# A gated delta-rule decoder layer with mixture of experts: one half of the batches runs 64 tokens ahead in the scan, and one pipeline takes all sixteen pairs

## Chip, cores and metric

One core of a Trainium2 chip. The metric is the device time of one execution in microseconds; the median of several runs counts.

## What is computed

The input x is 16 batches of 256 tokens of 256 features, all in f32. In the order of the reference:

1. RMS norm, a causal depthwise convolution over 4 tokens, SiLU, then projections to q, k, v (16 heads of 16) and to the gates beta and alpha.
2. The gated delta rule, token after token, per batch and head with a state S of 16 x 16: `S = a*S; pred = S.k; S = S + k (x) (beta*(v - pred)); o = S.q`. Only this part is serial in the tokens: token t needs S of token t-1.
3. Output projection and residual; RMS norm and a gated MLP with residual; layer norm of x plus all that.
4. Cross attention of the tokens over a context of 120 rows a batch, residual, layer norm.
5. A router picks one of 8 experts for each token; the expert is three matrices with two GELUs; residual, layer norm.

## The kernel before

**Units of work.** Tokens are cut into two blocks of 128 (jb 0 and 1). The batches are cut into two halves of eight (h 0 and 1), as one state instruction of VectorE holds 8 batches x 16 heads on its 128 partitions. A *pair* is two batches of one token block; there are sixteen, 0 to 7 in block 0 and 8 to 15 in block 1, of which 0 to 3 and 8 to 11 are half 0.

**The scan.** A half-token is one token of one half and takes four VectorE instructions: `state_product` (L135, S times k), `state_weights` (L147, the sum over the key axis, the value folded in as a 17th column), `state_outer` (L156), `state_update` (L166, writes S). Each needs the result of the one before it. `scan_step` writes them out by hand so that the two halves alternate: between two instructions of one half stands one of the other. The two halves share one buffer for the outer product, so the outer product of half 0 waits for half 1's update just ahead of it (a second semaphore, beside the one of its weights). `next_keys` (L113) copies four tokens of keys of both halves to PSUM, `next_values` (L118) two tokens of values of both halves. Eight tokens make a chunk (R = 8, 16 chunks a block); S of eight tokens is kept in a ring. GpSimd follows with `read_out` (L208 to L216): for four tokens of one half it multiplies S by q, folds the sum in three steps and writes the output over the values; the update waits for S to be read before it overwrites it. `store_o` sends a half's outputs of a block to memory.

**First block (front_and_scan).** PE, ScalarE, VectorE and GpSimd do part 1 for pairs 0 to 7; q, k, v and gates go through memory (`load_raw`) so that they come back with (batch, head) on the partitions. For each half VectorE then prepares: squares' sums (`sums`, L495), gates and inverse lengths (L475, L502), `normalise` of keys and queries (L513), `shares` (L480 to L486). With both halves prepared, the scan of block 0 runs: 128 tokens, all paired. Beside it the other engines do part 1 for pairs 8 to 15; `inverse_rms` of each on GpSimd stands between the read-outs of the chunks, so one pair goes with one chunk. Then the keys and values of the 16 contexts (`keys_values`). In the last two chunks VectorE does parts of the preparation of block 1; the rest stands behind the scan, since it writes into buffers that the scan reads.

**Second block (scan_and_post).** A pipeline of six stages over pairs: a mix and residual (L1088), b gate and up, f down and layer norm, c queries, scores and exponentials (VectorE: four maxima, L1113), d attention output and layer norm, e routing. In a step, stage a holds the newest pair. `PLAN = (1, 1, 1, 2, 2, 2, 2, 2, 1, 1, 1)` says how many chunks of the scan of block 1 VectorE does in each step, cut into turns of one token that stand between the stages' instructions. Pairs 0 to 7 enter in steps 0 to 7. Pairs 8 to 15 need the scan's end and enter in steps 11 to 18 (`AGAIN = M + 3`, M = 8). With the drain there are 24 steps. SP loads each pair's inputs (`load`), and for pair 8 and 9 first stores the two halves' outputs. Steps 5 to 7 and 16 to 18 are hardware loops, the others are written out.

**Then** a short block finishes the routing tables, and the experts run over 39 tiles of 128 rows; the change leaves both as they are, but for merged semaphores.

## Time and profile before

| | |
|---|---|
| median of 3 runs | 2015.93 us (2010.91 to 2018.14) |
| the profiled execution | 2012.56 us, its span 2010.9 us |
| busy over the span: PE, VectorE, GpSimd, ScalarE | 1408.4, 1274.6, 1000.1, 755.4 us |
| scan of block 0 | 118 to 537 us |
| scan of block 1 | 565 to 1085 us |
| last pair's residual | 1312 us |
| experts from | about 1460 us |

Busy time is that of instructions; VectorE's instructions overlap a little (the next can start before the last has ended), so its work is read best from start to start. The rows in order of time give start and duration in us, engine (DVE is VectorE, ACT ScalarE, POOL GpSimd, SP SyncE), line, operation, operands with shapes, and, in brackets, how long the engine was idle before and who ended it.

### The profile page before, as it was taken

How to read it: one execution, taken by the hardware profiler on the slowest of the kernel's cores; microseconds unless marked ns; L12 is line 12 of the kernel's file. 1: busy time of each engine (PE TensorE's matmuls, PEld its weight loads, DVE VectorE, ACT ScalarE, POOL GpSimd, SP SyncE). 2: the span in 40 equal slices, each digit the busy share in tenths (PEclk: the TensorE clock that was granted, in tenths of full speed). 3: DMA queues.
4: the chain of work that ended last, by engine and by line, in shares of the span. 5: the costliest groups of instructions: out<-in, count | busy, mean ns of one | idle time of the engine just before them, and what ended most of it. 6: DMA issues, size and time to landing. Idle time of an engine off the chain costs nothing. (4 is left out here: it accounts for less than half of the span.)

```text
span 2010.9 us, 28443 instructions
## 1 busy us (share of the span) xinstructions
PE 1408.4 (70%) x6660; PEld 977.0 (49%) x6661; DVE 1274.6 (63%) x3248; ACT 755.4 (38%) x2416; POOL 1000.1 (50%) x1214
## 2 busy tenths in 40 slices
PE   6504558600036676667766899998489999999997
PEld 4303336400024555545555677777345555555554
DVE  4599999999989999999986143443323223222222
ACT  5512224501103674566766577776311111111111
POOL 3238888886769987887766333341111111111111
PEclk9857778855557887878978999998789999999999
DMA  4601113610031011000002111143140420421200
GB/s 120 211 5 32 43 38 117 202 62 0 20 112 36 21 31 31 19 23 25 26 26 79 52 46 42 50 127 115 34 127 17 150 71 18 149 71 41 84 18 6
DMA packets 97685, 125.41 MB, mean 62 GB/s; under 512 B 10001, under 2 KB 74952, under 8 KB 95560
## 3 DMA queue, kind: packets, MB, share of 16 engines
q1 hardware_dynamic: 60040, 97.22, 15.3%
q10 hardware_dynamic: 33136, 18.58, 3.2%
q0 software_dynamic: 4432, 8.73, 1.2%
q8 instruction: 30, 0.49, 0.1%
q14 instruction: 47, 0.39, 0.1%
HBM read 89.68 MB, written 35.74 MB: 62 GB/s over the span
## 5 line engine op out<-in xcount | busy, mean ns | idle before, releaser
L208 POOL TENSOR_TENSOR wt<-wt 128x1024 f32<-128x1024 f32 x128 | 304.3, 2377 | 109.6 <-DVE wt L166 109.5
L214 POOL TENSOR_TENSOR wt<-wt 128x512 f32<-128x512 f32 (+2 forms) x384 | 316.9, 825 | 30.1
L1870 PE MATMUL e_ph<-wt,e_g 128*128 x624 | 274.3, 592 | 0.0
L166 DVE SCALAR_TENSOR_TENSOR wt<-wt,scan 128x256 f32<-128x256 f32 x512 | 242.2, 473 | 0.2 <-issue 0.2
L156 DVE TENSOR_TENSOR scan<-scan,wt 128x256 f32<-128x256 f32 x512 | 219.4, 429 | 20.1 <-DVE wt L166 14.0
L147 DVE TENSOR_REDUCE scan<-wt 128x16 f32<-128x272 f32 x512 | 222.6, 435 | 0.1
L135 DVE TENSOR_TENSOR wt<-wt,scan 128x256 f32<-128x256 f32 x512 | 209.5, 409 | 5.4 <-PEq L231 5.4
L1268 ACT ACTIVATE wt<-p_pX,p_mx 128x120 f32<-128x120 f32 x512 | 176.1, 380 | 89.3 <-DVE p_mx L1113 87.6
L1399 PE MATMUL p_pm<-p_w_mix,p_oT 128*128 128x256 f32 x128 | 43.5, 499 | 217.7 <-DMA p_oT<-o 188.6
L1763 POOL TENSOR_TENSOR e_ve<-e_mv,eps 128x1 f32<-128x1 f32 x39 | 7.4, 189 | 369.7 <-DVE e_mv L1814 369.7
L1870 PEld LDWEIGHTS e_ph<-wt,e_g 128*128 128x128 f32 x624 | 115.5, 190 | 130.8 <-issue 130.8
L1835 ACT ACTIVATE e_g<-e_pT 128x512 f32<-128x512 f32 x39 | 23.3, 597 | 337.9 <-PE e_pT L1885 337.9
L1908 PE MATMUL e_ph<-wt,e_xT 128*128 x312 | 149.4, 603 | 1.0 <-DVE e_xT L1785 1.0
L1792 DVE TENSOR_TENSOR e_h<-e_ph,wt 128x512 f32<-128x512 f32 x39 | 27.0, 692 | 183.4 <-PE e_ph L1870 183.4
L1399 PEld LDWEIGHTS p_pm<-p_w_mix,p_oT 128*128 128x128 f32 x128 | 30.5, 250 | 227.9 <-issue 221.4
L716 PE MATMUL f_pT<-ident,f_xn 128*128 128x128 f32 x64 | 14.9, 376 | 169.5 <-ACT f_xn L584 111.9
L1113 DVE TENSOR_REDUCE p_mx<-p_pX 128x8 f32<-128x960 f32 x64 | 72.9, 1149 | 89.0 <-PE p_pX L1442 88.8
L1410 PE MATMUL p_pX<-p_hT,p_wg 128*128 128x256 f32 (+1 forms) x384 | 108.3, 408 | 14.9 <-ACT wt L1268 14.9
L1800 DVE TENSOR_TENSOR e_h<-e_ph,wt 128x512 f32<-128x512 f32 x78 | 53.9, 692 | 101.4 <-PE e_ph L1908 99.6
L1420 PE MATMUL p_py<-p_wd,p_prod 128*128 128x256 f32 (+1 forms) x384 | 107.7, 427 | 12.5 <-DVE p_place L1168 9.1
L1268 ACT ACTIVATION_READ_ACCUMULATOR wt<-p_pX,p_mx 128x1 f32 x512 | 116.0, 226 | 0.0
L1410 PE MATMUL p_pX<-p_hT,p_wu 128*128 128x256 f32 (+1 forms) x384 | 103.0, 392 | 0.0
(220 smaller groups left out, 2977.2 us busy)
## 6 DMA issues: line engine op xcount, KB each, us to landing
wt<-in_L_ffn_W SPq DMA_DIRECT2D x24, 1024.0 KB
qkv<-f_st ACTq DMA_DIRECT2D x48, 256.0 KB, 2.3
p_kE<-kE SPq DMA_DIRECT2D x16, 480.0 KB, 3.7
p_vP<-vP SPq DMA_DIRECT2D x16, 480.0 KB
e_xt<-routed ACTq DMA_DIRECT2D x39, 130.0 KB, 2.1
f_xt<-in_x SPq DMA_DIRECT2D x16, 256.0 KB, 2.8
f_raw_k<-qkv SPq DMA_DIRECT2D x4, 1024.0 KB, 6.0
f_raw_q<-qkv SPq DMA_DIRECT2D x4, 1024.0 KB, 8.2
```

The source lines that it names most:

```text
L135: nc.vector.tensor_tensor(s["sk"][:, h, u % V, :, 0:HD], s["S"][:, h, (u - 1) % R], s["kn"][:, h, u % KN:u % KN + 1].to_broadcast([P, HD, ...
L147: nc.vector.tensor_reduce(s["w"][:, h], s["sk"][:, h, u % V], AX, ALU.add).then_inc(s["w_done"], 1)
L156: nc.vector.tensor_tensor(s["outer"][:], s["w"][:, h].rearrange("p (v o) -> p v o", o=1).to_broadcast([P, HD, HD]), s["k"][:, h, bass.ds(c ...
L166: nc.vector.scalar_tensor_tensor(s["S"][:, h, u], s["S"][:, h, (u - 1) % R], s["gate"][:, jb, h, 1, bass.ds(c * R + u, 1)], s["outer"][:], ...
L208: nc.gpsimd.tensor_tensor(x, s["S"][:, h, z * Q:(z + 1) * Q], s["q"][:, h, now].rearrange("p t (o d) -> p t o d", o=1).to_broadcast([P, Q, ...
L214: nc.gpsimd.tensor_tensor(x[:, :, :, 0:half], x[:, :, :, 0:half], x[:, :, :, half:2 * half], ALU.add).then_inc(s["o_fold"][h], 1)
L1268: ins = nc.scalar.activation(pr[:, x // 2, head], scores(x)[:, y // 4, y % 4], ACT.Exp, bias=mx[:, x // 2, head:head + 1], accum_out=sm[:, ...
L1399: ins = nc.tensor.matmul(dst[:, q], rows[:, g, q * P:(q + 1) * P], wt[:, g], start=(g == 0), stop=(g == G - 1))
L1410: ins = nc.tensor.matmul(gu(i)[0:c, which], wt[:, g, i * P:i * P + c], hT[:, g], start=(g == 0), stop=(g == G - 1))
L1420: ins = nc.tensor.matmul(py[:, q], prod[0:c, i, q * P:(q + 1) * P], wd[0:c, i], start=(i == 0), stop=(i == IC - 1))
L1870: ins = nc.tensor.matmul(ph2[:], g1[:, c // (C1 // 2), c % (C1 // 2)], wt[:, bass.ds(at_b + (W2_AT + c * F2), F2)], start=(c == 0), stop=( ...
L1908: ins = nc.tensor.matmul(ph1[:, q], xT[:, g], wt[:, bass.ds(at + (W1_AT + g * F1 + q * HALF), HALF)], start=(g == 0), stop=(g == G - 1))
```

## The change

Half 0 begins its scan as soon as it is prepared, alone (`one_step`: the four instructions of one half-token in a row). Half 1 is prepared between those steps and begins when half 0 is at token 64 (`LEAD` = 8 chunks); from then on `pair_step` alternates the two as before, half 0 at token t + 64 and half 1 at t. Since half 0 finishes a block 64 tokens before half 1, its inputs for block 1 must be there by then while the buffers still hold block 0: the preparation of block 1 writes to the freed raw buffers, `keep_next` stores that to memory (new tensor `next`) and `load_next` brings it back when the half's scan of block 0 is over. For half 0 this happens at the end of the first block, beside 8 tokens of half 1 alone, for half 1 in step 3 and 4 of the second block.

The second block does two slots of the scan (a slot is a chunk of either or both halves) in each of steps 0 to 11: slots 0 to 6 hold both (block 1 of half 0, the rest of block 0 of half 1), slot 7 half 0 alone, slots 8 to 15 both, slots 16 to 23 half 1 alone. Pairs 8 to 11 (half 0) enter in steps 8 to 11 and pairs 12 to 15 from step 12; `AGAIN` is M, and with the drain there are 21 steps. Semaphores of the scan are kept per half, key and value refills are per half and each for four tokens, and several semaphores that counted one instruction each are merged into their neighbours' (`ms_done` into `rstd_done`, `st_done` into `mv_done`, `ve_done` into `rs_done`, in all blocks), with the same instructions and waits.

The diff's core:

```diff
+LEAD = CHUNKS // 2
...
-def scan_step(nc, dve, s, jb, vo, c, u, last=False):
-    t = c * R + u
-    behind = (c, u - 1) if u else (c - 1, R - 1)
-    begun = not (isinstance(c, int) and c == 0 and u == 0)
-    state_product(nc, dve, s, jb, c, u, 0)
-    if begun:
-        state_outer(nc, dve, s, jb, *behind, 1)
-    state_weights(nc, dve, s, jb, c, u, 0)
-    if begun:
-        state_update(nc, dve, s, jb, *behind, 1)
-        if u % 2 == 0 and not (last and u == R - 2):
-            next_values(nc, s, vo, t + 2, (u - 2) % V, 2)
-    state_outer(nc, dve, s, jb, c, u, 0)
-    state_product(nc, dve, s, jb, c, u, 1)
-    state_update(nc, dve, s, jb, c, u, 0)
-    if u % KN == KN - 1 and not (last and u == R - 1):
-        dve.wait_ge(s["sk_done"], (c + jb * CHUNKS) * (2 * R) + (2 * u + 2))
-        next_keys(nc, s, t + 1)
-    state_weights(nc, dve, s, jb, c, u, 1)
...
+def updated(dve, s, at):
+    h, jb, c, u = at
+    dve.wait_ge(s["S_done"][h], (c + jb * CHUNKS) * R + (u + 1))
+def refill_keys(nc, dve, s, at):
+    h, jb, c, u = at
+    if u % KN == KN - 1 and not (isinstance(c, int) and c * R + u == TB - 1):
+        dve.wait_ge(s["sk_done"][h], (c + jb * CHUNKS) * R + (u + 1))
+        next_keys(nc, s, h, c * R + (u + 1))
+def refill_values(nc, dve, s, at):
+    h, jb, c, u = at
+    if u % V == V - 1 and not (isinstance(c, int) and c * R + u == TB - 1):
+        dve.wait_ge(s["w_done"][h], (c + jb * CHUNKS) * R + (u + 1))
+        next_values(nc, s, h, c * R + (u + 1))
+def one_step(nc, dve, s, at):
+    state_product(nc, dve, s, at)
+    refill_keys(nc, dve, s, at)
+    state_weights(nc, dve, s, at)
+    refill_values(nc, dve, s, at)
+    state_outer(nc, dve, s, at)
+    state_update(nc, dve, s, at)
+def pair_step(nc, dve, s, lead, follow, begins=False, ends=False):
+    h, jb, c, u = follow
+    behind = (h, jb, c, u - 1) if u else (h, jb, c - 1, R - 1)
+    state_product(nc, dve, s, lead)
+    if not begins:
+        state_outer(nc, dve, s, behind)
+    state_weights(nc, dve, s, lead)
+    if not begins:
+        state_update(nc, dve, s, behind)
+    refill_values(nc, dve, s, lead)
+    if not begins:
+        updated(dve, s, behind)
+    state_outer(nc, dve, s, lead)
+    state_product(nc, dve, s, follow)
+    state_update(nc, dve, s, lead)
+    refill_keys(nc, dve, s, lead)
+    refill_keys(nc, dve, s, follow)
+    state_weights(nc, dve, s, follow)
+    refill_values(nc, dve, s, follow)
+    if ends:
+        updated(dve, s, lead)
+        state_outer(nc, dve, s, follow)
+        state_update(nc, dve, s, follow)
+        updated(dve, s, follow)
...
+def load_next(sp, s, k, h):
+    sp.wait_ge(s["S_done"][h], TB)
+    sp.dma_start(s["k"][:, h].rearrange("p t d -> p (t d)"), k["next"][h, 0]).then_inc(s["next_in"][h], 16)
+    sp.wait_ge(s["S_read"][h], 2 + TB // Q)
+    sp.dma_start(s["q"][:, h].rearrange("p t d -> p (t d)"), k["next"][h, 1]).then_inc(s["next_in"][h], 16)
+    store_o(sp, s, k, 0, h)
+    sp.wait_ge(s["o_out"][h], 16)
+    sp.dma_start(s["vo"][:, h].rearrange("p d t -> p (d t)"), k["next"][h, 2]).then_inc(s["next_in"][h], 16)
...
+            def keep_next(h):
+                sp.wait_ge(norm_done, 4 + 2 * h + 1)
+                sp.dma_start(k["next"][h, 0], raw_v[:, h].rearrange("p d t -> p (d t)")).then_inc(next_out, 16)
+                sp.wait_ge(next_out, 48 * h + 16)
+                load_values(1, h, raw_v)
+                sp.wait_ge(norm_done, 4 + 2 * h + 2)
+                sp.dma_start(k["next"][h, 1], raw_k[:, h].rearrange("p d t -> p (d t)")).then_inc(next_out, 16)
+                sp.wait_ge(next_out, 48 * h + 32)
+                sp.wait_ge(share_done, shared(2 + h, VALUED))
+                sp.dma_start(k["next"][h, 2], raw_v[:, h].rearrange("p d t -> p (d t)")).then_inc(next_out, 16)
+                sp.wait_ge(next_out, 48 * h + 48)
             load_rows(0)
             for h in range(2):
                 load_raw(0, h)
+                load_values(0, h, s["vo"])
             load_rows(1)
+            for h in range(2):
+                load_raw(1, h)
...
+            for a in range(2):
+                lead_outputs(a)
             for a in range(2):
                 inverse_rms((M + a, a, M // 2))
-                outputs(a)
             with pool.Fori(0, M // 2 - 1) as i:
                 for u in range(2):
                     inverse_rms((i * 2 + (M + 2 + u), u, i + (M // 2 + 1)))
-                    outputs(i * 2 + (2 + u))
-            with pool.Fori(M, CHUNKS) as c:
-                outputs(c)
+                    lead_outputs(i * 2 + (2 + u))
+            pool.wait_ge(norm_done, 4)
+            with pool.Fori(0, LEAD) as c:
+                both_outputs(c)
+            for z in range(R // Q):
+                read_out(nc, pool, s, 1, 0, LEAD, z)
...
+            def halves(jb, h):
+                keys, queries, gates, inverse, shares = lengths(jb, h)
+                return [keys, queries, gates, inverse, partial(normalise, jb, h, 0), partial(normalise, jb, h, 1), shares]
+            parts = halves(0, 1)
+            for c in range(2):
+                for u in range(R):
+                    one_step(nc, dve, s, (0, 0, c, u))
+                    if c * R + u in (3, 5, 6, 8, 9, 10, 12):
+                        parts.pop(0)()
+            with dve.Fori(2, LEAD) as c:
+                for u in range(R):
+                    one_step(nc, dve, s, (0, 0, c, u))
             dve.wait_ge(share_done, shared(1, VALUED))
             dve.wait_ge(norm_done, 4)
-            dve.wait_ge(parity_done, 4)
-            scan_start(nc, s, values[0])
-            scan_chunk(nc, dve, s, 0, values[0], 0)
-            with dve.Fori(1, CHUNKS - 2) as c:
-                scan_chunk(nc, dve, s, 0, values[0], c)
+            updated(dve, s, (0, 0, LEAD - 1, R - 1))
+            scan_start(nc, s, 1)
+            for u in range(R):
+                pair_step(nc, dve, s, (0, 0, LEAD, u), (1, 0, 0, u), begins=u == 0)
+            with dve.Fori(1, LEAD - 4) as c:
+                for u in range(R):
+                    pair_step(nc, dve, s, (0, 0, c + LEAD, u), (1, 0, c, u))
             for h in range(2):
-                parts = list(lengths(1, h))
-                for u in range(R):
-                    scan_step(nc, dve, s, 0, values[0], CHUNKS - 2 + h, u, last=h == 1)
-                    if u in (1, 2, 4, 6, 7):
-                        parts.pop(0)()
-            dve.wait_ge(s["S_done"], 2 + 2 * TB)
-            for h in range(2):
-                normalise(1, h, 0)
-            for h in range(2):
-                dve.wait_ge(s["S_read"][h], 2 + TB // Q)
-                normalise(1, h, 1)
-            dve.wait_ge(share_done, shared(3, VALUED))
-            dve.wait_ge(norm_done, 8)
-            scan_start(nc, s, values[1])
+                parts = halves(1, h)
+                for x in range(2):
+                    c = LEAD - 4 + 2 * h + x
+                    for u in range(R):
+                        pair_step(nc, dve, s, (0, 0, c + LEAD, u), (1, 0, c, u), ends=c == LEAD - 1 and u == R - 1)
+                        if x * R + u in (0, 2, 3, 5, 7, 9, 14):
+                            parts.pop(0)()
+            for u in range(R):
+                one_step(nc, dve, s, (1, 0, LEAD, u))
+            updated(dve, s, (1, 0, LEAD, R - 1))
+            dve.wait_ge(s["next_in"][0], 48)
+            scan_start(nc, s, 0)
...
-    PLAN = (1, 1, 1, 2, 2, 2, 2, 2, 1, 1, 1)
-    AGAIN = M + 3
+    AGAIN = M
+    GROUP = M // 2
...
+                until = start + M - (1 - jb)
+                with eng.Fori(start + DEPTH - 1, until) as step:
                     body(jb, step)
-                first = start + M
+                first = until
...
+            def during(slot):
+                if not isinstance(slot, int) or LEAD <= slot < 2 * LEAD:
+                    return (0, 1, slot), (1, 1, slot - LEAD)
+                if slot < LEAD - 1:
+                    return (0, 1, slot), (1, 0, slot + (LEAD + 1))
+                return ((0, 1, slot) if slot < LEAD else (1, 1, slot - LEAD)), None
+            if jb or isinstance(step, int) and step >= 3 * GROUP:
+                return []
+            return [during(step * 2 + i) for i in range(2)]
...
+                    if isinstance(a, int) and a == GROUP:
+                        load_next(sp, s, k, 1)
                     for h in range(2):
-                        if isinstance(a, int) and a == M + h:
-                            store_o(sp, s, k, 1, s["vo"], h)
-                        if isinstance(a, int) and a == M + h * (M // 2):
+                        if isinstance(a, int) and a == M + h * GROUP:
+                            store_o(sp, s, k, 1, h)
                             sp.wait_ge(s["o_out"][h], 32)
...
+                    (x, y), u = turns[i]
+                    if y is None:
+                        one_step(nc, dve, s, (*x, u))
+                    else:
+                        fresh = isinstance(step, int) and step in (0, GROUP) and i == 0
+                        final = isinstance(step, int) and (step, i) in ((GROUP - 1, R - 1), (2 * GROUP - 1, 2 * R - 1))
+                        pair_step(nc, dve, s, (*x, u), (*y, u), begins=fresh, ends=final)
+                    if isinstance(step, int) and (step, i) == (GROUP - 1, 2 * R - 1):
+                        updated(dve, s, (*x, u))
+                        dve.wait_ge(s["next_in"][1], 48)
+                        scan_start(nc, s, 1)
```

## Rows read from the trace of the kernel before

**Rows 1.** Busy us of each engine by stage, columns named in the first line.

```profile
core 0: us, PE busy (x) PEld busy (x) DVE busy (x) ACT busy (x) POOL busy (x), PEclk, DMA share, GB/s
733.00:800.00 67.00, 45.75 (x250) 35.17 (x249) 64.54 (x168) 37.78 (x136) 51.72 (x61) 0.81 0.09 27
1190.00:1227.00 37.00, 36.62 (x248) 29.30 (x244) 14.77 (x31) 28.01 (x104) 13.99 (x20) 1.00 0.18 49
```

**Rows 2.** VectorE in order of time: start, duration, line, operands; paired scan, loop.

```profile
141.35 0.29 DVE L113 COPY scan<-wt 128x128 f32<-128x128 f32 x1
...
153.37 0.47 DVE L166 SCALAR_TENSOR_TENSOR wt<-wt,scan 128x256 f32<-128x256 f32 x1
153.76 0.28 DVE L113 COPY scan<-wt 128x128 f32 x1
153.95 0.43 DVE L147 TENSOR_REDUCE scan<-wt 128x16 f32<-128x272 f32 x1
154.30 0.41 DVE L135 TENSOR_TENSOR wt<-wt,scan 128x256 f32<-128x256 f32 x1
...
164.62 0.47 DVE L166 SCALAR_TENSOR_TENSOR wt<-wt,scan 128x256 f32<-128x256 f32 x1
165.28 0.43 DVE L156 TENSOR_TENSOR scan<-scan,wt 128x256 f32<-128x256 f32 x1 [0.18 <-DVE wt L166]
...
166.34 0.29 DVE L113 COPY scan<-wt 128x128 f32 x1
```

**Rows 3.** The same view, scan instructions that wait for the one ahead.

```profile
118.25 0.41 DVE L135 TENSOR_TENSOR wt<-wt,scan 128x256 f32<-128x256 f32 x1
118.70 0.45 DVE L147 TENSOR_REDUCE scan<-wt 128x16 f32<-128x272 f32 x1
119.18 0.43 DVE L156 TENSOR_TENSOR scan<-scan,wt 128x256 f32<-128x256 f32 x1
...
536.37 0.43 DVE L156 TENSOR_TENSOR scan<-scan,wt 128x256 f32<-128x256 f32 x1
536.84 0.48 DVE L166 SCALAR_TENSOR_TENSOR wt<-wt,scan 128x256 f32<-128x256 f32 x1
```

**Rows 4.** The same view, the score maximum of half a step, two steps apart.

```profile
733.62 1.15 DVE L1113 TENSOR_REDUCE p_mx<-p_pX 128x8 f32<-128x960 f32 x1
...
867.77 1.15 DVE L1113 TENSOR_REDUCE p_mx<-p_pX 128x8 f32<-128x960 f32 x1
```

**Rows 5.** VectorE's last scan instruction; all residuals; two loads one step apart.

```profile
1084.04 0.48 DVE L166 SCALAR_TENSOR_TENSOR wt<-wt,scan 128x256 f32<-128x256 f32 x1
...
L1088 DVE TENSOR_TENSOR p_h<-p_pm,p_xt x16: 680/691/694, 583.4 to 1311.6; 128x512 f32<-128x512 f32 x16
...
1236.08 0.37 SPq L942 DMA_DIRECT2D p_oT<-o  x1
...
1273.80 0.37 SPq L942 DMA_DIRECT2D p_oT<-o  x1
```

**Rows 6.** VectorE in order of time: half 1's preparation begins; the next scan's first product.

```profile
96.05 1.94 DVE L495 TENSOR_TENSOR wt<-wt 128x1024 f32<-128x1024 f32 x2
...
565.06 0.42 DVE L135 TENSOR_TENSOR wt<-wt,scan 128x256 f32<-128x256 f32 x1 [5.41 <-PEq L231]
```

**Rows 7.** GpSimd in order of time, two read-outs running one after the other.

```profile
129.36 2.35 POOL L208 TENSOR_TENSOR wt<-wt 128x1024 f32<-128x1024 f32 x1 [14.15 <-DVE wt L166]
...
134.64 2.34 POOL L208 TENSOR_TENSOR wt<-wt 128x1024 f32<-128x1024 f32 x1
```

**Rows 8.** DMA issues by line: operands, count, size, median us to landing.

```profile
o<-f_vo SPq DMA_DIRECT2D x2, 1024.0 KB, 3.9
```

**Rows 9.** VectorE in order of time, a small operation on two SBUF operands.

```profile
758.32 1.89 DVE L1150 TENSOR_TENSOR p_best<-p_lg,p_lmax 128x16 f32<-128x16 f32 x1
```

**Rows 10.** ScalarE's norm and next squares; SP's load behind the contexts.

```profile
203.24 0.91 ACT L584 ACTIVATE f_xn<-f_xt,f_rstd 128x256 f32<-128x256 f32 x2 [10.34 <-POOL f_rstd L401]
...
218.18 0.42 ACT L577 ACTIVATE f_xn<-f_xt 128x256 f32<-128x256 f32 x1 [2.38 <-issue]
...
391.97 0.36 SPq L344 DMA_DIRECT2D f_raw_k<-qkv  x1
```

More of the change, by code:

```diff
@@ L202, in read_out @@
+def read_out(nc, pool, s, h, jb, c, z):
     g = c + jb * CHUNKS
@@ L603, in step @@
                     if jb:
-                        nc.scalar.activation(xT[:, slot, :, :, 0:KC - 1], tail[:, pair].rearrange("p m g q t -> p (m g) q t"), ACT.Copy).then_inc(halo_done, 1)
+                        nc.scalar.activation(xT[:, slot, :, :, 0:KC - 1], tail[:, pair].rearrange("p m g q t -> p (m g) q t"), ACT.Copy)
                     for g in range(G):
@@ L1179, in step @@
                 on, a, b, f, c, d, e = at(jb, step)
-                turns = [(x, u) for x in chunks(jb, step) for u in range(R)]
+                turns = [(halves, u) for halves in chunks(jb, step) for u in range(R)]
                 def scan(i):
-                    if len(turns) < 2 * R:
-                        if i % 2 or not turns:
-                            return
-                        i //= 2
-                    x, u = turns[i]
-                    scan_step(nc, dve, s, 1, s["vo"], x, u, last=isinstance(x, int) and x == CHUNKS - 1)
+                    if not turns:
+                        return
+                    (x, y), u = turns[i]
[9 more added lines that the diff above has]
+                        scan_start(nc, s, 1)
                 if "d" in on and late(jb, d):
```

286 lines of the change are left out of this document (134 added, 152 removed).

## The prediction, made before the changed kernel had run

> **What bounds the kernel now.** I read the page's busy shares first, then the busy time by stage, then VectorE's instructions in order of time, last the waits at the joints. Over the whole span PE is the busiest engine and VectorE the second, but that is a mean over two regimes, which only the table by stage parts. While the scan runs, VectorE is busy 64.5 us of 67 in a step of the pipeline; with the scan over, it is PE, 36.6 us of 37 [rows 1]. So VectorE sets the time from about 97 us to 1084 us, PE from there on, and the question is how much work and waiting each stretch holds after the change.
>
> A token of both halves costs 3.12 us: eight tokens lie between the key copy at 141.35 and the one at 166.34 [rows 2]. In that order each instruction's forerunner belongs to the other half, and the next starts before the last has ended: the reduce at 153.95 is followed after 0.35 us by a product, though it lasts 0.43 us. (Looking at the ends of the rows alone would hide that: each start counts.) The one tight spot is the outer product that must wait for the update just in front of it (they share one buffer): 0.66 us from start to start at 164.62, against 0.39 us for the update at 153.37 in front of a key copy [rows 2].
>
> **The change, part by part.** The scan's amount stays: 512 half-tokens. Before they are 256 tokens of two halves. After, I count from the diff 64 (chunks 0 to 7 of half 0) + 8 (chunk 8 of half 1 alone) + 8 (slot 7) + 64 (slots 16 to 23) = 144 half-tokens alone and 184 pairs.
>
> *A, the alone steps.* In one_step each instruction needs the one right ahead. Such starts are in the trace: product to reduce 0.45 us, reduce to outer product 0.48 us, outer product to update 0.47 us [rows 3]; update to product isn't there, I take its duration and the same 0.04 us of pause, 0.51 us. Together 1.91 us. Every four tokens a key and a value refill come in, 0.19 us each by the copy at 153.76 [rows 2]: 0.09 us a token. Three instructions in four tokens wait on two semaphores; the update before such a wait takes 0.66 us in place of 0.51 [rows 2], so 0.11 us a token. That is 2.1 us where half a paired token costs 1.56 us. 144 x 0.54 = **+78 us**. Bounds: 1.91 + 0.04 (144 x 0.39 = 56 us) to 2.2 (92 us).
>
> The rows show a reduce followed after 0.35 us without a wait on it [rows 2] and after 0.48 us with one [rows 3]; such differences make this term, and I keep the rows' price. The Trainium skill, "VectorE: DVE Perf Modes", section "The DRAIN you can't avoid", says otherwise: the next operation can't start until the pipe is empty in any case, and the semaphore costs nothing extra. By that the term would be 0; this case's trace does not agree with it.
>
> *B, the paired steps.* Key copies are now one per half, so one more in four tokens, 0.19 us if the half-size copy is no cheaper, 0.1 if it is; value refills stay two in four tokens, but the lead's fills the gap behind an update once where it was filled twice, +0.27 us (0.66 - 0.39); and the follower's refill waits for the reduce ahead of it, +0.13 us (0.48 - 0.35 [rows 2, 3]). About 0.5 us in four tokens; 46 x 0.5 = **+23 us** (0 to 28).
>
> *C, pipeline work that now lies inside the scan.* A full step lasts 67.1 us (two steps between 733.62 and 867.77 [rows 4]), 16 tokens of it 50.0, so all stages together cost VectorE 17 us. Before, stages a, f, c, d, e run 8, 8, 8, 7, 6 times until the scan ends; after, 12, 10, 9, 8, 7 times. One full set, three more residuals at 0.7 (their median [rows 5]), one more f with its statistics and one multiplication by the reciprocal sums, which by their sizes beside a residual I estimate at 2 us each: **+23 us** (20 to 26).
>
> *D, the tail.* Now the last scan instruction starts at 1084.04 and the last pair's residual at 1311.6 [rows 5]: 227 us, in which pairs 8 to 15 enter an emptied pipeline. After, pair 11 is in when the scan ends (step 11), and pairs 12 to 15 follow. Steps without scan take 37.7 us (1236.08 to 1273.80 [rows 5]), and step 12's residual comes 30 us behind the scan's end (37.7 less the 12 us of scanning behind the residual of step 11 would be 26; I add some for PE, which starts the step late). 30 + 3 x 37.7 = 143: **-84 us** (-90 to -76). What follows the last residual, routing and experts included, is unchanged.
>
> *E, the front.* Half 0's scan starts at the folds of 96.05 in place of 118.25 [rows 3, 6], and half 1's preparation, these 22 us, moves between its steps: no work is saved. The four normalisations and the last shares go from behind the scan into it, again the same work. At the joint VectorE waits 5.4 us today before 565.06 [rows 6]. After it, half 0's next keys, queries and values come back from memory: behind half 0's last update GpSimd must read out one quad of four tokens or two, at 5.3 us each (129.36 to 134.64 [rows 7]), then come a store of 3.9 us to landing [rows 8] and a load of the same size, taken at 5, some 20 us with the issues, against 8 alone tokens of 17 us; and the block ends only when GpSimd has read out the last alone quad, 5.3 us and the barrier: 8.5 us, +3. The moved operations read two SBUF operands while GpSimd works on SBUF; the same kind shows 1.89 us for 16 elements there [rows 9], so the moved ones lose some too, +2 (0 to 15), as they are few and long. Sum: **+5 us**.
>
> Does the front feed this? A pair takes 15 us from its norm to the next pair's squares (203.24 to 218.18 [rows 10]), a chunk alone 16.8 us, so the pairs are paced as fast as the scan asks and the projections end some 45 us earlier. The contexts end at 391.97 today [rows 10], some 350 after (391.97 less the 45). Half 0's new preparation begins after 16 + 48 tokens alone and 32 paired: 97 + 134 + 22 + 104 = 357. Cover is 7 us; if ScalarE is later, VectorE waits for its squares by that much.
>
> *F, the hand-overs inside the pipeline.* load_next for half 1 sits on SP in step 4 ahead of the loads of that step; half 1 ends at turn 7 of step 3, and the same chain (GpSimd's read-out, which stands behind inverse_std and biased, then store and load) takes some 25 us against 22 us of slot 7 and stage work: 3 us. Pair 8 waits for half 0's store in the same manner, hidden by 25 us of step 8. Steps 8 to 11 need 34 + 17 = 51 us of VectorE against 37.7 for PE, so they stay VectorE's. With 2 us for coupling that is 5 us, less 4 us for shorter waits on GpSimd, whose read-outs are halved in steps 8 to 11: **+1 us** (-6 to 20).
>
> The merged semaphores change what is counted, not how many waits there are: 0. Four scan_start calls in place of two are hidden by nothing and cost two refills of 0.19 us each, under 1 us in all. GpSimd is busy 51.7 of 67 us in a full step [rows 1] and stays under VectorE, whose step grows.
>
> Sum: 78 + 23 + 23 - 84 + 5 + 1 = +46. The profiled execution took 2012.56 us (span 2010.9); that gives 2058.6. The median of the runs, 2015.93, lies 3.4 above it: **2062 us**.
>
> **Rivals.** (1) *Waits cost nothing*: alone steps cost what half a pair costs and the refills hide. Then A and B fall away and the time is 2062 - 101 = 1961 us, faster. It decides in one_step and turns if an alone token costs under 1.78 us (46/144 = 0.32 less). Against it stand the starts in [rows 3]; for it, that no alone token as a whole is in the trace. Chance 0.07. The rule of the Trainium skill cited under A ("VectorE: DVE Perf Modes") is this rival's. (2) *Half the added cost*: alone tokens at 1.95, cheap refills, a tail of 137 us and 6 us less at the joints: 2062 - 22 - 12 - 6 - 6 = 2016, no change. Chance 0.08. (3) *Late feeding*: the contexts end 15 us later than I say, and both reloads (next_in) are late by 10 us more; the time goes to VectorE's waits, not its work: 2062 + 35 = 2097. For it speaks the thin cover of 7 and 3 us. Chance 0.12. (4) The change does not do what it says, the leading half waiting for the other: then pairs 8 to 11 would not be ready in step 8; the counts in the diff leave no room for it, 0.01, and it would be slower too. My forecast keeps 0.72.
>
> **How the numbers follow.** About 0.5% is what a measurement of this kernel can tell from no change, 10 us. Range: low end 2062 less A's and B's lower bounds in part (22 + 15) = 2025, which leaves most of rivals 1 and 2 out; high end with A at 92, the contention at 15 and 7 us of late feeding, 2092. Faster 0.09 (rival 1 and 0.02 of 2), same 0.08 (the rest of 2 and 0.02 of the forecast's low fringe), slower 0.83 (0.70 + 0.12 + 0.01).
>
> **What would show it.** Right: VectorE's busy count unchanged for its four scan lines (512 each), alone stretches with starts of 0.45 to 0.51 us, 2.1 us a token; pairs at 3.25 us; the next block's first scan product near 529 us; scan end near 1217 us; the last residual 140 to 150 us later; steps 8 to 11 at some 51 us. Wrong: an alone token under 1.8 us, or residuals of steps 8 to 11 less than 45 us apart, which would take VectorE off the path; or a VectorE wait of more than 10 us for squares, next_in or a read-out, which would be rival 3.

## The result, and the profile after

The changed kernel takes **2046.31 us** (median of four runs, 2045.61 to 2048.45). The kernel before, run again beside it, takes 2016.88 (2010.91 to 2018.14). The ratio is 1.0158, with a 95% interval from 1.0141 to 1.0174: slower by 1.6%, clear of the spread of the runs, and 16 us less slow than forecast. The profiled execution of the changed kernel took 2048.45 us (the slowest of the four), its span is 2046.2 against 2010.9, so the two traces lie 35 us apart and the medians 29.

The page's busy times, with the columns of section 1, and then its groups of VectorE's four scan lines (busy us, mean ns of one, idle us before them and what ended most of it):

```profile
span 2046.2 us, 28245 instructions
PE 1411.9 (69%) x6660; PEld 979.2 (48%) x6661; DVE 1340.8 (66%) x3314; ACT 758.7 (37%) x2418; POOL 1003.5 (49%) x1214
...
L164 DVE SCALAR_TENSOR_TENSOR wt<-wt,scan 128x256 f32<-128x256 f32 x512 | 243.4, 475 | 16.0 <-POOL wt L235 5.6
L153 DVE TENSOR_TENSOR scan<-scan,wt 128x256 f32<-128x256 f32 x512 | 219.5, 429 | 17.1 <-DVE wt L164 5.8
L146 DVE TENSOR_REDUCE scan<-wt 128x16 f32<-128x272 f32 x512 | 223.9, 437 | 3.8
L135 DVE TENSOR_TENSOR wt<-wt,scan 128x256 f32<-128x256 f32 x512 | 210.3, 411 | 16.2 <-PEq L269 8.3
```

The four counts are still 512, and one instruction lasts as long as before (473, 429, 435 and 409 ns there). The idle time in front of the four grew from 25.8 us in all to 53.1. The rest of the loss is not written there at all: an instruction that starts while its forerunner still runs shares its time with it, so busy sums hide the loss. It shows only in the starts.

VectorE in order of time, first in the front's alone steps that are written out, then in the loop behind them (chunks 2 to 7), then the end of the scan:

```profile
97.58 0.41 DVE L135 TENSOR_TENSOR wt<-wt,scan 128x256 f32<-128x256 f32 x1
98.02 0.45 DVE L146 TENSOR_REDUCE scan<-wt 128x16 f32<-128x272 f32 x1
98.50 0.43 DVE L153 TENSOR_TENSOR scan<-scan,wt 128x256 f32<-128x256 f32 x1
98.97 0.48 DVE L164 SCALAR_TENSOR_TENSOR wt<-wt,scan 128x256 f32<-128x256 f32 x1
99.49 0.42 DVE L135 TENSOR_TENSOR wt<-wt,scan 128x256 f32<-128x256 f32 x1
...
176.67 0.48 DVE L164 SCALAR_TENSOR_TENSOR wt<-wt,scan 128x256 f32<-128x256 f32 x1 [5.64 <-POOL wt L235]
...
184.14 0.42 DVE L135 TENSOR_TENSOR wt<-wt,scan 128x256 f32<-128x256 f32 x1
...
188.32 0.42 DVE L135 TENSOR_TENSOR wt<-wt,scan 128x256 f32<-128x256 f32 x1
188.77 0.45 DVE L146 TENSOR_REDUCE scan<-wt 128x16 f32<-128x272 f32 x1
189.38 0.43 DVE L153 TENSOR_TENSOR scan<-scan,wt 128x256 f32<-128x256 f32 x1 [0.16 <-DVE scan L146]
189.96 0.48 DVE L164 SCALAR_TENSOR_TENSOR wt<-wt,scan 128x256 f32<-128x256 f32 x1
...
193.14 0.42 DVE L135 TENSOR_TENSOR wt<-wt,scan 128x256 f32<-128x256 f32 x1
...
536.74 0.42 DVE L135 TENSOR_TENSOR wt<-wt,scan 128x256 f32<-128x256 f32 x1 [8.25 <-PEq L269]
...
1195.82 0.48 DVE L164 SCALAR_TENSOR_TENSOR wt<-wt,scan 128x256 f32<-128x256 f32 x1
```

All residuals of the changed kernel, in the view of one tile's instructions (durations in ns, first and last start in us):

```profile
L1165 DVE TENSOR_TENSOR p_h<-p_pm,p_xt x16: 680/684/692, 569.5 to 1346.1; 128x512 f32<-128x512 f32 x16
```

Written out, an alone token takes 1.91 us from product to product (97.58 to 99.49), with starts 0.44, 0.48, 0.47 and 0.52 apart: the sum of [rows 3]. In the loop four tokens take 9.00 us (184.14 to 193.14), 2.25 each, refills included. There the reduce is followed by the outer product after 0.61 us (188.77 to 189.38) in place of 0.48, and that by the update after 0.58 in place of 0.47. The instructions that start later are those whose address or count comes from the loop's variable. In front of nearly each of them (42 of the 48 outer products) stands a register operation of VectorE's own sequencer (DVEq), which the rows in order of time leave out. The view of line 153 has it, over the loop of the alone steps:

```profile
L153 DVEq FUSED_REGOPS  x42: 69/75/82, 152.3 to 264.2; - x42
```

For the outer product at 189.38 it starts at 189.3, behind the end of the reduce (188.77 + 0.45 = 189.22), and takes 0.075 us. In the steps that are written out there is none.

The table by stage of the changed kernel, columns as in [rows 1]; steps 5 and 6 in part, then steps 8 to 11, then a step without scan:

```profile
866.00:933.00 67.00, 43.48 (x248) 34.27 (x248) 62.40 (x171) 37.79 (x136) 49.80 (x57) 0.83 0.09 27
999.00:1196.00 197.00, 162.89 (x992) 129.57 (x992) 178.71 (x405) 142.26 (x511) 134.82 (x166) 0.90 0.13 42
1227.00:1265.00 38.00, 37.60 (x251) 29.99 (x250) 15.17 (x32) 29.02 (x108) 14.04 (x20) 1.00 0.18 51
```

Steps 8 to 11 are a regime of its own: VectorE is busy 179 of 197 us and PE 163. They follow each other by 46.9 to 50.4 us (residuals at 1038.12, 1084.98, 1132.39, 1182.79 and the next at 1232.87). Once the scan is over, PE is the bound as before, 37.6 of 38 us.

**Where the time went.** I added VectorE's starts (from each instruction to the next) between marks that both traces have, idle times over 0.9 us kept apart. From the first scan product to the last scan update, the scan's lines and refills take 868.3 us against 789.8 (+78.5); all other work 202.3 against 158.0 (+44.3, of which 22.7 is half 1's preparation, that lay ahead of the scan before, so the scan also starts 20.7 us earlier: 97.58 against 118.25); waits over 0.9 us 27.6 against 18.0 (+9.6). 78.5 + 44.3 + 9.6 - 20.7 = +111.7, which is the move of the last update from 1084.04 [rows 5] to 1195.82. From there to the last residual it is 150.3 us against 227.6, -77.3. Together +34.4, and the last residual is indeed at 1346.1 against 1311.6 (34.5 apart).

### The profile page after: what moved, and what is told of

It is laid out like the page before. It is cut to its first block and busy times, and to the rows that moved or that the text cites. A ratio compares the mean times of both kernels' runs of the same rounds, so it can differ in the third digit from the quotient of the medians.

```text
span 2046.2 us, 28245 instructions
## 1 busy us (share of the span) xinstructions
PE 1411.9 (69%) x6660; PEld 979.2 (48%) x6661; DVE 1340.8 (66%) x3314; ACT 758.7 (37%) x2418; POOL 1003.5 (49%) x1214
## 5 line engine op out<-in xcount | busy, mean ns | idle before, releaser
L241 POOL TENSOR_TENSOR wt<-wt 128x512 f32<-128x512 f32 (+2 forms) x384 | 323.8, 843 | 30.1
L1504 PE MATMUL p_py<-p_wd,p_prod 128*128 128x256 f32 (+1 forms) x384 | 115.1, 450 | 20.8 <-POOL p_prod L1104 8.1
L1352 ACT ACTIVATION_READ_ACCUMULATOR wt<-p_pX,p_mx 128x1 f32 x512 | 114.5, 224 | 0.0
L1504 PEld LDWEIGHTS p_py<-p_wd,p_prod 128*128 128x128 f32 (+1 forms) x384 | 79.2, 220 | 54.7 <-issue 43.9
```

The lines of the kernel that those rows point to most:

```text
L241: nc.gpsimd.tensor_tensor(x[:, :, :, 0:half], x[:, :, :, 0:half], x[:, :, :, half:2 * half], ALU.add).then_inc(s["o_fold"][h], 1)
L1352: ins = nc.scalar.activation(pr[:, x // 2, head], scores(x)[:, y // 4, y % 4], ACT.Exp, bias=mx[:, x // 2, head:head + 1], accum_out=sm[:, ...
L1504: ins = nc.tensor.matmul(py[:, q], prod[0:c, i, q * P:(q + 1) * P], wd[0:c, i], start=(i == 0), stop=(i == IC - 1))
```

## The experiments

**Is an alone step dear because of its order?** The first question is A, the largest term. The most direct test leaves the changed kernel aside and alters the order alone, in the kernel before. For that its loops had to be written out first (the loop body needs one order), which is an experiment of its own.

```diff
-            with dve.Fori(1, CHUNKS - 2) as c:
+            for c in range(1, CHUNKS - 2):
                 scan_chunk(nc, dve, s, 0, values[0], c)
...
-            steps(dve, step)
+            steps(dve, step, unrolled=True)
```

> The kernel before with its two loops of VectorE written out in the same way (the scan's chunks 1 to 5 of the first block, and pipeline steps 5 to 7). If a loop's addresses cost time in the order of before too, its paired half-tokens go from 1.55 to about 1.50 us: 0.05 x 80 + 0.05 x 96 = 9 us, and the joints of the loop in the pipeline some 4 to 8 more: 2016 - 15 = 2001 us, range 1998 to 2008, which beats both kernels. Rival: in the order of before the gaps between dependent instructions are filled by the other half, so a later start costs nothing there: 2013 to 2018 us. The second rival also says that the changed kernel owes part of its loss to the loops, the first that both kernels pay them alike.

Measured: 2006.33 us beside 2013.94 for the kernel before on the same chip, ratio 0.996 (0.9945 to 0.9975). The expectation miscounted: the first loop holds chunks 1 to 13, 208 half-tokens and not 80. Per half-token the scan there went from 1.546 to 1.519 us, half of what the first theory said; the later block gave 4.1 us more, in the pipeline's loop. The time lies in the first theory's range (1998 to 2008), near its slow end. So a later start costs little in the order of before, not nothing: the other half stands between most dependent instructions. What changed is the one start that does wait on its forerunner, that of the outer product behind the other half's update. In the loop it is 0.66 us at 164.62 [rows 2] (0.65 at the median of 51); written out it is 0.58, in VectorE's order of time:

```profile
165.37 0.47 DVE L166 SCALAR_TENSOR_TENSOR wt<-wt,scan 128x256 f32<-128x256 f32 x1
165.95 0.43 DVE L156 TENSOR_TENSOR scan<-scan,wt 128x256 f32<-128x256 f32 x1
```

An outer product behind a product it doesn't wait on starts after 0.33 us in both, with the register operation in front or without. The kernel is 7.6 us faster than before and 40 faster than the changed one, the best version of this study. In its trace the scan's lines take 779.9 us against 789.8, but VectorE's waits over 0.9 us grow from 18.0 to 24.0, so the last residual comes 4.9 us sooner (1306.8).

On it the order was changed in the first block. A new `serial_step` takes the place of `scan_step` (refills are left out here, at the "..."):

```diff
+def serial_step(nc, dve, s, jb, vo, c, u, leave=False):
+    for h in range(2):
+        n = (c + jb * CHUNKS) * (2 * R) + (2 * u + h + 1)
+        if h == 0:
+            dve.wait_ge(s["S_done"], n + 1)
+        state_product(nc, dve, s, jb, c, u, h)
+        ...
+        state_weights(nc, dve, s, jb, c, u, h)
+        if h == 1:
+            ...
+            dve.wait_ge(s["S_done"], n + 1)
+        state_outer(nc, dve, s, jb, c, u, h)
+        state_update(nc, dve, s, jb, c, u, h)
+        ...
...
+            for t in range(R + 1, (CHUNKS - 2) * R):
+                serial_step(nc, dve, s, 0, values[0], t // R, t % R, leave=t == (CHUNKS - 2) * R - 1)
```

> b_unroll with one thing changed: in 39 tokens of the first block (chunk 1 from its second token to chunk 5) the four instructions of one half run one behind the other, then the four of the other half, in place of the interleaved order; the work, the tokens and everything outside stay. The product of the leading half is given a wait on the instruction right ahead, that of the other half none, so one trace shows both. Theory (what an alone step costs is the wait on its forerunner): 78 half-tokens at 1.85 to 1.95 us in place of 1.50, so +27 to +35 us against b_unroll, and the start of a product 0.45 to 0.50 us behind an update where it waits on it, 0.33 to 0.40 where it does not. The rule of the Trainium skill (VectorE: DVE Perf Modes, The DRAIN you can't avoid), that the semaphore costs nothing extra: the two starts are alike, and the kernel takes the time of b_unroll within 5 us. Rival in between (the alone steps are slow because of their refills and of loops, not of order): +5 to +15 us.

The count is wrong here too: it is 103 tokens, 206 half-tokens, from chunk 1 to chunk 13, so the theory's 0.35 to 0.45 us for each come to 72 to 93 us. The range as written, 27 to 35, was missed; the price for each half-token held. Measured: 2095.71 us, ratio to before 1.0397 (1.0377 to 1.0417), 89 us over the version with the old order. VectorE in order of time:

```profile
201.14 0.48 DVE L166 SCALAR_TENSOR_TENSOR wt<-wt,scan 128x256 f32<-128x256 f32 x1
201.66 0.42 DVE L135 TENSOR_TENSOR wt<-wt,scan 128x256 f32<-128x256 f32 x1
202.11 0.45 DVE L147 TENSOR_REDUCE scan<-wt 128x16 f32<-128x272 f32 x1
202.59 0.43 DVE L156 TENSOR_TENSOR scan<-scan,wt 128x256 f32<-128x256 f32 x1
203.06 0.48 DVE L166 SCALAR_TENSOR_TENSOR wt<-wt,scan 128x256 f32<-128x256 f32 x1
203.46 0.41 DVE L135 TENSOR_TENSOR wt<-wt,scan 128x256 f32<-128x256 f32 x1
...
649.72 0.42 DVE L135 TENSOR_TENSOR wt<-wt,scan 128x256 f32<-128x256 f32 x1 [5.40 <-PEq L252]
```

The product at 201.66 (half 0) waits for the update ahead of it and starts 0.52 us behind it; the product at 203.46 (half 1) has no such wait and starts 0.40 us behind the same kind of update. So it is all through the stretch: 0.51 to 0.52 in 96 starts with the wait, 0.40 in 49 without. The two also belong to different halves, and the first has a second wait, long since reached; but the changed kernel has the same 0.52 with one wait (98.97 to 99.49), and the run `free` below has 0.39 for the same half without. So 0.12 us is the price of a wait on the forerunner. In all, a half-token takes 1.95 us against 1.519, 0.43 x 206 = 89 us, and the next block's first product moves from 560.70 to 649.72, by the same 89. The Trainium skill's rule, cited in the prediction ("VectorE: DVE Perf Modes", "The DRAIN you can't avoid", where it is told of a chain of copies), would have left both the 0.12 and the 89 us at zero; this case's traces do not agree with it for these instructions.

**What would the change give if these waits were gone?** In the changed kernel the alone steps were given operands that do not hang on the instruction ahead. For that the outer product also moves in front of the reduce, and the value refill behind the update.

```diff
-    state_product(nc, dve, s, at)
...
+    state_product(nc, dve, s, at, 1)
+    state_outer(nc, dve, s, at, 1)
     refill_keys(nc, dve, s, at)
     state_weights(nc, dve, s, at)
+    state_update(nc, dve, s, at)
     refill_values(nc, dve, s, at)
-    state_outer(nc, dve, s, at)
-    state_update(nc, dve, s, at)
```

> The changed kernel with the wait on the forerunner taken out of the alone steps: the product reads the state two tokens back, the outer product takes the weights of the token before from a second buffer, and the value refill comes after the update. Same instructions, sizes, counts and places; the recurrence of the alone tokens is computed from older values, so the outputs differ from the reference's. Theory (the wait on the forerunner is the price of the alone steps): starts of 0.33 to 0.39 us, 1.5 to 1.6 us an alone half-token; the front loses 24 x 0.4 + 48 x 0.7 = 43 us of work, of which up to 17 us come back as waits on GpSimd, as chunks of 12.4 us meet pairs of 15.3 us; slot 7 loses 4 us; steps 8 to 11 lose 26 us if VectorE bounds them: 1975 to 1990 in all. If the pipeline's other engines hold steps 8 to 11 at 47 us anyway, these 26 us stay and it is 2000 to 2015. Rival (hand-overs through memory and contention are the price): within 10 us of 2046.

Measured: 2024.27 us, ratio 1.0045 (1.0030 to 1.0060), 22 us less than the changed kernel. That is outside both ranges of the theory (1975 to 1990, 2000 to 2015) and below the rival's. VectorE in order of time, then the update's group of the page, then the residuals:

```profile
139.60 0.41 DVE L137 TENSOR_TENSOR wt<-wt,scan 128x256 f32<-128x256 f32 x1
139.93 0.42 DVE L157 TENSOR_TENSOR scan<-scan,wt 128x256 f32<-128x256 f32 x1
140.27 0.43 DVE L148 TENSOR_REDUCE scan<-wt 128x16 f32<-128x272 f32 x1
140.61 0.47 DVE L168 SCALAR_TENSOR_TENSOR wt<-wt,scan 128x256 f32<-128x256 f32 x1
141.00 0.41 DVE L137 TENSOR_TENSOR wt<-wt,scan 128x256 f32<-128x256 f32 x1
...
167.84 0.48 DVE L168 SCALAR_TENSOR_TENSOR wt<-wt,scan 128x256 f32<-128x256 f32 x1 [10.71 <-POOL wt L246]
...
715.26 0.23 DVE L112 COPY scan<-wt 128x64 f32<-128x64 f32 x1 [5.64 <-DMA wt<-next]
```

```profile
L168 DVE SCALAR_TENSOR_TENSOR wt<-wt,scan 128x256 f32<-128x256 f32 x512 | 241.2, 471 | 29.2 <-POOL wt L246 28.9
```

```profile
L1176 DVE TENSOR_TENSOR p_h<-p_pm,p_xt x16: 679/682/694, 548.4 to 1318.5; 128x512 f32<-128x512 f32 x16
```

The same four operations now take 1.40 us a token (139.60 to 141.00) where they took 1.91. The theory's price was right: over the 144 alone half-tokens the scan's lines and refills take 216.0 us for 293.6, 78 us less of VectorE's time, and the whole scan's 791.9 us are those of the kernel before (789.8). But the last residual comes only 28 us earlier, since waits over 0.9 us grow by 44 (27.6 to 71.9). What stands next in line takes it: 28.9 us of updates that wait for GpSimd to read out the ring of eight states (5.64 in the changed kernel), 9.4 us at the two reloads of the values (3.75 at 507.64 and 5.64 at 715.26; 2.10 before), and steps 8 to 11. There the scan's lines give back 27 us (121.8 to 95.1), yet the residuals still follow each other by 45 to 49 us for 47 to 50, as waits on PE's results (score maxima, placements) grow from 7.7 to 21.8. So even with A at nothing the change would not have been faster than before: the forecast's rival 1 was wrong in its price and also in what it would have brought.

**The loops.** Two runs wrote VectorE's loops of the changed kernel out, first that of the alone steps, then all three.

```diff
-            with dve.Fori(2, LEAD) as c:
+            for c in range(2, LEAD):
```

> The changed kernel with VectorE's loop over chunks 2 to 7 of half 0 written out instruction by instruction; nothing else. In the changed kernel's trace an alone half-token costs 2.27 us in that loop and 1.95 us where it is written out. Theory (waiting for the instruction one ahead is the price, and a loop only adds to it): 48 x 0.32 = 15 us less than the changed kernel's 2046, so about 2031, with starts of 0.45 to 0.51 us everywhere in the stretch and 1.95 us a half-token left, still 0.4 us above half a paired token. Rival (the loop's address registers are the price, not the wait for the forerunner): the alone half-token falls to 1.55 us, 2012 or less. Rival (the pairs' pace holds the scan there, GpSimd's read-outs stand behind the mean squares of a pair each 15.3 us): VectorE's time goes into waits on GpSimd and the kernel stays within 5 us of 2046.

Measured: 2040.82 us, ratio 1.0118 (1.0100 to 1.0136), 5.5 us less than the changed kernel: a third of what the theory wanted, far from the first rival (2012 or less) and just outside the second (within 5 us). The 48 tokens go from 114.5 to 104.7 us, and 8.0 us of waits over 0.9 us on GpSimd are in there, 6.62 of them at 176.02, where the changed kernel had 5.64. Without them a half-token costs 2.27 us in the loop and 2.01 written out; of the 12 us won there, 2.4 went into those waits, so the second rival is right for a part.

```diff
-            with dve.Fori(1, LEAD - 4) as c:
+            for c in range(1, LEAD - 4):
...
-            steps(dve, step)
+            steps(dve, step, unrolled=True)
```

> The changed kernel with all three of VectorE's hardware loops written out: the alone stretch of the front (as in u_alone), the paired stretch behind it, and pipeline steps 5 and 6. Nothing else differs. Theory (an instruction behind a wait starts about 0.12 us later where its address comes from the loop's variable): against the changed kernel's 2046 us, the alone stretch gives up to 15 us of which u_alone kept 6 to 9; the paired stretch, 1.62 to 1.66 us a half-token in loops against 1.51 to 1.53 written out, gives some 0.11 x 24 tokens x 2 = 5 us more in the front and 0.13 x 32 tokens x 2 = 8 us in steps 5 and 6, and the 2.9 to 5 us of issue at the loop's joint near 860 us go: 2046 - 6 - 5 - 8 - 4 = 2023, range 2018 to 2032. Rival (the loops' cost is covered by other waits, the time comes back as waits on GpSimd): 2036 to 2041, as u_alone.

Measured: 2032.27 us, ratio 1.0088 (1.0070 to 1.0107), 14 us less than the changed kernel (11 less if each is taken against the kernel before that ran beside it, 16 between the two traces). That lies between the theory's 23 and the rival's 5 to 10, at the very end of the theory's range. Paired half-tokens went from 1.62 to 1.54 in the front and from 1.61 to 1.53 in steps 5 and 6, where 2.88 us of idle time at the loop's joint (867.35) went too. VectorE's waits in the front, and the next block:

```profile
175.70 0.48 DVE L164 SCALAR_TENSOR_TENSOR wt<-wt,scan 128x256 f32<-128x256 f32 x1 [6.85 <-POOL wt L235]
...
241.93 0.48 DVE L164 SCALAR_TENSOR_TENSOR wt<-wt,scan 128x256 f32<-128x256 f32 x1 [1.60 <-POOL wt L235]
...
525.90 0.42 DVE L135 TENSOR_TENSOR wt<-wt,scan 128x256 f32<-128x256 f32 x1 [7.74 <-PEq L269]
```

Both kernels fully written out stand at 2032.27 and 2006.33, a ratio of 1.0129. So the loops carry less than a quarter of the change's loss (26 of 29 to 30 us are left without them, 14.0 - 7.6 = 6 at most are theirs). The rest belongs to what both versions of the change share: the order of the alone steps, against the moved stage work and the shorter tail.

**GpSimd's wait in the front.** At 176.67 VectorE waits 5.64 us for a read-out that GpSimd does late. GpSimd in order of time, of the changed kernel:

```profile
161.56 0.20 POOL L456 TENSOR_TENSOR f_ms<-f_ss,eps 128x2 f32<-128x2 f32 x1 [3.97 <-ACT f_xn L655]
...
173.17 0.20 POOL L456 TENSOR_TENSOR f_ms<-f_ss,eps 128x2 f32<-128x2 f32 x1 [10.65 <-ACT f_xn L655]
173.45 0.69 POOL L458 TENSOR_TENSOR f_rstd<-f_ms,exponent 128x2 f32<-128x2 f32 x1
174.10 2.36 POOL L235 TENSOR_TENSOR wt<-wt 128x1024 f32<-128x1024 f32 x1
```

It stands 10.65 us at the statistics of a pair whose squares aren't there, with the read-out at 174.10 queued behind. The first two chunks' read-outs stand ahead of all statistics there, so three pairs' statistics follow one another. One run puts the statistics of pair 8 ahead of chunk 0's read-outs and those of pair 9 ahead of chunk 1's.

```diff
             for a in range(2):
+                inverse_rms((M + a, a, M // 2))
                 lead_outputs(a)
-            for a in range(2):
-                inverse_rms((M + a, a, M // 2))
```

> The changed kernel with GpSimd's first four pieces in another order: inverse_rms of pair 8, read-outs of chunk 0, inverse_rms of pair 9, read-outs of chunk 1, in place of both read-outs first. In the changed kernel's trace GpSimd waits 10.65 us for pair 10's squares before it reads out chunk 2, and VectorE stands 5.64 us at 176.67 for it. Theory (that stall is VectorE's own time): 5 to 8 us less, 2038 to 2041, and the wait is gone. Rival (the time comes back in the next chunks or at the joint of the two blocks): no difference above 2 us.

Measured: 2046.49 us, ratio 1.0154 (1.0140 to 1.0168), the changed kernel's time. The wait has moved, to 4.03 us at 124.22, and the next block starts 3.8 us sooner (532.99), as does the last residual, but the median shows nothing of it. So the rival's forecast (no difference above 2 us) stands. Only this one order of GpSimd's queue was tried, and it didn't take the wait away.

**Do pairs 8 to 11 pay inside the scan?** The tail is shorter because they run in steps 8 to 11 while the follower still scans. This run holds them back three steps.

```diff
-    AGAIN = M
+    AGAIN = M + 3
```

> The changed kernel with the pipeline as it was: pairs 8 to 15 enter from step 11 (AGAIN = M + 3), the scan's slots stay where they are, in steps 0 to 11. This prices the half of the change that gives something. Theory (the tail lost 77 us and 20 us of stage work moved into the scan): three steps of 37.7 us more behind the scan, less some 30 us of work that steps 8 to 11 no longer hold: 60 to 90 us above 2046, 2105 to 2135. Rival (the early entry gives little, as steps 8 to 11 are held by their own stages, and the whole loss is in them): less than 40 us more, under 2086.

Measured: 2077.53 us, ratio 1.0305 (1.0289 to 1.0322), 31 us over the changed kernel, below what the theory wanted and in the rival's range. The last scan update in order of time, then the residuals:

```profile
1168.10 0.48 DVE L164 SCALAR_TENSOR_TENSOR wt<-wt,scan 128x256 f32<-128x256 f32 x1
```

```profile
L1165 DVE TENSOR_TENSOR p_h<-p_pm,p_xt x16: 678/683/692, 570.5 to 1374.8; 128x512 f32<-128x512 f32 x16
```

From the last update to the last residual it is 207 us in place of 150, so the tail grows by 57; but the scan ends 28 us earlier (1168.10 for 1195.82), since fewer stages run beside it and its last steps are only 41 to 45 us apart. Pairs that start inside the scan pay about two to one: what they take from the tail is the larger part, and half of it is spent again on VectorE in the longer steps.

## Why the prediction was right, and where its sizes were off

The sign, the order of the terms and the mechanism held: 2062 was forecast, 2046.3 came, inside the range of 2025 to 2092. The net of the forecast was +46 us on the profiled execution and +34 on the last residual was measured. In part that is luck: A and B were too high by 22 us together, the tail and the waits too favourable by 12. The high end of the range is also added up wrongly: 2062 with 14 more for A, 13 for contention and 7 for late feeding is 2096, not 2092. Term by term:

**A, the alone steps, +78 forecast, +72 measured.** Without waits over 0.9 us the 144 half-tokens took 293.6 us, 2.04 each, against 1.543 (789.8 / 512) on the mean before. The price of starts that wait on their forerunner was read rightly from [rows 3]; update to product, which had to be put together, was given 0.51 and is 0.52. The 2.1 us are near the mean for a partly wrong reason: written out it is 1.95 with refills in the first 16 and 2.01 over the long stretch of `u_alone`, since the extra 0.11 us for waits on two semaphores is mostly not there, while in the loop it is 2.27 by the late addresses. The starts of [rows 3] come from code that is written out. The one dependent start that I read from a loop, 0.66 us in [rows 2], I put down to its second semaphore alone; written out it is 0.58, so about half of the 0.15 us was the loop's.

**B, the paired steps, +23 forecast, +7 measured.** This is the term that was furthest off. (868.3 - 293.6) / 368 is 1.562 us a half-token against 1.543; with both kernels written out it is 1.537 against 1.523, +5. The key copy of one half is cheap (0.14 us to the next start at 191.05 in the trace of the changed kernel, not 0.19). I priced each moved refill by the dearest neighbour in [rows 2] and took 0.5 us of a range from 0 to 28 us in all, near its high end. Which of the moved refills came cheaper than priced wasn't tried one by one.

**C, stage work inside the scan, +23 forecast (and 2 for contention under E), +24 measured**: 44.3 us more of other work, less the 20.7 us that lay ahead of the scan. The moved operations lose nothing that shows.

**D, the tail, -84 forecast, -77 measured.** Three steps of 37.4 to 38.2 us came as written. The term that was off is the first: step 12's residual comes 37 us behind the scan's end (1195.82 to 1232.87), not 30. I had subtracted part of a scan step from it as if PE were ahead; PE, busy 163 of 197 us in steps 8 to 11, had little in hand, as it seems; no run tried that by itself.

**E, the front, next block forecast at 529, measured at 536.74.** The joint is as forecast (8.25 us for 8.5). The alone stretch is 12 us longer, 97.58 to 265.83, 168 us where I had 134 + 22 = 156, by the loop's late starts and the 5.64 us on GpSimd; behind it some 4 us are won back, the pairs being cheaper. I had asked whether the front feeds the squares of half 0's next preparation, and it did (no such wait is in the trace). I had not asked whether GpSimd's queue, where read-outs stand behind a pair's statistics, would hold the ring of eight states. That is a wait of the same family as rival 3, in another place.

**F, hand-overs, +1 forecast.** All waits over 0.9 us, joints included, grew by 9.6 us, where F and the joint under E made 4: new are 5.64 on GpSimd, 2.8 more at the joint (8.25 for 5.41), 2.88 at the end of the pipeline's loop, and 2.10 at the reload for half 1, where I had 3. Waits on PE's results are a little smaller than before (8.7 us for 10.4; 5.52 and 2.21 of them in step 8).

Steps 8 to 11 were forecast at 51 us and came at 47 to 50, by the cheaper alone steps (1.90 a half-token there); the scan's end, forecast at 1217, came at 1195.82 for the same reason and for B.

**The rivals.** Rival 1 fell by the 1.91 us and the two starts of 0.52 and 0.40. Rival 2, half the added cost, named the true price of a written-out alone token and the cheap refills, but expected a shorter tail and joints than came; the result lies between it (2016) and the forecast, two thirds of the way to the forecast. Rival 3 didn't come: the waits on reloads are 2.1 us. The change did what it says.

What stays open: why steps 8 to 11 don't fall below 45 to 49 us when their alone steps are cheaper was seen in waits on PE's results but wasn't tried by itself.

## What to carry to other kernels

Where one engine sets the time, work can only be moved under its cover if its own stream stays as dense: taking the interleaved partner away from 144 of 512 half-tokens cost 72 us of VectorE's time, nearly as much as the earlier start of half the pairs saved in the tail (77). Price a chain of dependent instructions from start to start, never by busy sums, and read the starts from the same kind of code (written out or in a loop) as the change will run. Before counting on a faster stretch, ask what its next limit is: of 78 us freed in the alone steps, 22 reached the end.

## What the runs showed of the hardware that wasn't expected

- In a hardware loop an instruction of VectorE that waits on its forerunner and takes an address or count from the loop's variable started 0.58 to 0.61 us behind it; written out, 0.45 to 0.48. The register operation of VectorE's sequencer starts only when the forerunner has ended (189.3 behind a reduce that ends at 189.22) and the instruction behind that. Where the instruction doesn't wait on its forerunner the register operation costs nothing that shows: product to outer product is 0.33 us in the kernel before, in its loop and written out. In alone steps the loop cost 0.25 us a token (2.27 against 2.01 over the same 48), in interleaved ones 0.03 a half-token in the order of before (1.546 against 1.519) and 0.08 in the changed kernel's pairs.
- Which of two waits ahead of one instruction is the late one shows. In the run with the serial order, the outer product of half 0 started 0.48 us behind the reduce it waits on (202.11 to 202.59, and so in 102 starts), that of half 1 0.55 us (200.12 to 200.67, 101 starts). Both also wait on a semaphore long since reached. In the kernel's text the wait on the reduce stands first for half 0 and second for half 1; in the trace the second one is an instruction of the sequencer by itself:

```profile
L155 DVEq EVENT_SEMAPHORE  x1: 21/21/21, 202.1 to 202.1; - x1
...
L153 DVEq EVENT_SEMAPHORE  x1: 21/21/21, 200.6 to 200.6; - x1
```

  At 202.1 that is the wait that is already reached, done before the reduce has ended. At 200.6 it is the wait on the reduce, and the outer product follows it. The halves differ here too, so the order of the waits wasn't tried by itself.
- The Trainium skill, "Perfetto Trace Analysis", section "DVE / Act Engine Instruction (TENSOR_ADD, Activation, etc)", tells for VectorE that the next instruction may begin its prefetch when the last has finished executing; a wait on its semaphore is served later, at the write's acknowledgement. The 0.40 against 0.52 us above fit that, without proving where in the pipe the 0.12 us lie.
